# A Mamba block and six local-attention layers in one kernel: the loads of x at the head, the second norm inside the scan, the final sums inside the last layer's slots

## What is computed

```python
# Mamba block, d_inner 256, 16 states
xz, x_gate = x @ W_in + b_in, x @ W_gate + b_gate
act = silu(causal_conv4(xz) + conv_b)
delta = softplus(act @ W_delta + b_delta); Bm, Cm = act @ W_B, act @ W_C
h[t] = exp(delta[t] * A) * h[t-1] + (delta[t] * act[t]) * Bm[t]     # for each channel and state
y[t] = sum_n h[t] * Cm[t] + act * D_skip
x1 = (y * silu(x_gate)) @ W_out + b_out

# six layers, 16 heads of 64, windows of 32 tokens that look one window back
x = attn_layer(shift_tokens(x), ...) + x
x = ffn_layer(shift_tokens(x), ...) + x      # layer norm, W1, gelu gate, W2
```

## Time and profile before

| | us |
|---|---|
| median of three runs | 3793.05 |
| lowest and highest run | 3788.48, 3798.14 |
| the profiled execution: its time | 3797.34 |
| the profiled execution: its span in the trace | 3795.5 |
| from the span's start to the first input projection (PE) | 55.90 |
| first layer's first copy of `xT` (ACT) | 672.93 |
| last `add_y` (DVE) begins | 3779.60 |

### The profile page before, as it was taken

How to read it: one execution, slowest core, us unless ns; L and a number is a source line. 1 busy time by engine, 2 the same in 40 slices (tenths; PEclk the granted TensorE clock), 3 DMA queues, 4 the chain that set the end, 5 groups by cost and what they waited for, 6 DMA issues and landing times.

```text
span 3795.5 us, 148907 instructions
## 1 busy us (share of the span) xinstructions
PE 3526.2 (93%) x61280; PEld 2227.8 (59%) x61280; DVE 3139.4 (83%) x4377; ACT 2647.5 (70%) x4972; POOL 2423.3 (64%) x2197
## 2 busy tenths in 40 slices
PE   5677676899999999999999999999999999999997
PEld 2222222466666666666666666666666666666664
DVE  4899998788888888888878888788888888888883
ACT  4545454677777777777777777777777777777775
POOL 0356555676666666666667676667676666666661
PEclk9889899899999999999999999999999999999998
DMA  3000000011111111111111111011111111111111
GB/s 78 0 0 0 0 0 0 26 34 30 32 37 49 37 32 32 32 49 37 37 33 32 43 43 38 28 32 32 49 41 34 32 32 49 38 37 32 32 32 34
DMA packets 64426, 120.18 MB, mean 32 GB/s; under 512 B 18196, under 2 KB 35986, under 8 KB 63634
## 3 DMA queue, kind: packets, MB, share of 16 engines
q1 hardware_dynamic: 63762, 110.70, 10.0%
HBM read 20.50 MB, written 2.10 MB: 6 GB/s over the span
## 4 chain that ended last, share of the span: by engine, by line
POOL 32%; issue 26%; PE 23%; DVE 1%; ACT 1%; POOLq 1%; DMA 0%; DVEq 0%; ACTq 0%; SPq 0%
POOL arena L501 18%; POOL arena L508 8%; POOL arena L515 6%; PE qk L1132 5%; PE trb L1004 3%; PE ob L1193 3%; PE vob L1201 3%; PE vob L1138 2%; PE sc L1220 2%; PE sc L1169 2%; PE ob L1004 1%; PE sc L1227 1%; PE sc L1163 0%; PE vob L1243 0%; POOL arena L484 0%
## 5 line engine op out<-in xcount | busy, mean ns | idle before, releaser
L508 POOL TENSOR_TENSOR arena<-arena,rnorm 128x512 f32<-128x512 f32 x768 | 786.5, 1046 | 904.0 <-ACT rnorm L627 903.4
L501 POOL TENSOR_TENSOR arena<-arena 128x512 f32<-128x512 f32 x768 | 963.9, 1278 | 36.5 <-DVE arena L889 36.4
L634 ACT ACTIVATE arena<-trb 128x512 f32<-128x512 f32 x768 | 462.6, 602 | 412.9 <-PE trb L1004 412.8
L1132 PE MATMUL qk<-wqkv,xs 128*128 128x512 f32 x1536 | 732.6, 600 | 17.9 <-issue 10.6
L888 DVE TENSOR_TENSOR arena<-qk,tab_q 128x512 f32<-128x512 f32 x384 | 263.5, 686 | 414.7 <-ACT arena L620 407.3
L484 POOL TENSOR_TENSOR arena<-arena 128x512 f32<-128x512 f32 x256 | 300.3, 1183 | 344.3 <-DVE arena L860 328.8
L1004 PE MATMUL trb<-ident,arena 128*128 128x128 f32 x3072 | 483.8, 280 | 14.6 <-ACT arena L634 6.9
L1132 PEld LDWEIGHTS qk<-wqkv,xs 128*128 128x128 f32 x1536 | 293.8, 192 | 311.6 <-issue 295.6
L894 DVE TENSOR_REDUCE ssq<-arena 128x16 f32<-128x1024 f32 x384 | 463.9, 1208 | 0.0
L620 ACT ACTIVATE arena<-qk 128x512 f32<-128x512 f32 x768 | 426.9, 587 | 46.7 <-PE qk L1132 34.1
L1004 PEld LDWEIGHTS trb<-ident,arena 128*128 128x128 f32 x3072 | 347.2, 141 | 147.0 <-issue 99.2
(11 more groups left out here) (139 smaller groups left out, 5862.5 us busy)
## 6 DMA issues: line engine op xcount, KB each, us to landing
arena<-arena SPq DMA_DIRECT2D x192, 384.0 KB, 3.2
arena<-arena SPq DMA_DIRECT2D x192, 64.0 KB, 3.0
wqkv<-in_L_ffn_Wqkv SPq DMA_DIRECT2D x18, 512.0 KB, 3.7
wo<-in_L_ffn_Wo SPq DMA_DIRECT2D x6, 512.0 KB, 5.5
arena<-in_L_attn_x SPq DMA_DIRECT2D x8, 256.0 KB, 2.8
out<-arena SPq DMA_DIRECT2D x8, 256.0 KB, 2.2
w<-in_L_ffn_W SPq DMA_DIRECT2D x6, 341.0 KB, 3.0
arena<-in_sel SPq DMA_DIRECT2D x1, 1024.0 KB, 5.2
```

Of the source, the lines that this page charges most:

```text
L501: nc.gpsimd.tensor_tensor(ts[c * 2 + j][:, heads], tu[:, 0, heads], tu[:, 1, heads], ALU.add).then_inc(summed[0], 1)
L508: nc.gpsimd.tensor_tensor(part, part, rnorm[j][:, 8 * h:8 * h + 8].unsqueeze(2).to_broadcast([P, 8, HEAD]), ALU.mult) \
L634: A((qT, kT)[j][u][:, 4 * h:4 * h + 4, at_col:at_col + P], TRB.rearrange("p (a t) -> p a t", a=4), ACT.Copy) \
L1132: MM(QK[:, 512 * h:512 * h + 512], lhsT=xs[u][:, c * P:(c + 1) * P], rhs=wqkv[:, col:col + 512], start=True, stop=True) \
```

## The change

- **Load.** The identity matrix has a semaphore of its own (`ident_in`) and is loaded first; x follows in eight loads without any wait, each to its own place (`x_tokens`, in the space of `act[0]`) with its own semaphore. The other 25 parameter loads come after. PE waits for the identity and for each block, turns block g into PSUM bank g; the waits for `const_in` move to the first instruction that needs a parameter. ACT's Exp for `a_neg` moves behind the first norm.
- **Second norm.** `NORM_AT` = 14. In the scan of group g the norm of block g - 1 is made in single instructions: `mean_of` on PE at the end of state 13, `centre_output` on DVE at the start of state 14, `square_of` on ACT after the exponentials of state 14, `var_of` on PE after state 15's first step, `root_of` (Ln, Exp) on ACT after the last exponential, `scale_output` on DVE after `gate(g)`. All use bank 7 and one buffer each (`pxc`, `psq`, `prstd`). Only block 7 is left for after the scan.
- **Finish.** `FINAL` names eight slots of the last layer; at the end of such a slot each engine also does its step of `finish` for one block. The buffers are `sq[0]` and `tu`, free after the last unit. From slot 79 on ACT does not load the Exp table again after a gelu (`drain`).

The diff, cut to its core (counts of items shift by 8 where the norms' semaphores lose the second norm's items: that is left out):

```diff
+FINAL = {67: 0, 68: 1, 69: 2, 70: 3, 71: 4, 74: 5, 80: 6, 86: 7}
...
-    for k in range(TURN, LAYER - PER_GROUP + LAG_DOWN + 1):
+    for k in range(TURN, max(FINAL) + 1):
         body(DEPTH - 1, k)
...
-        OUT_AT, D_AT, Z_AT, BC_AT = 2, 5, 9, 13
+        OUT_AT, D_AT, Z_AT, BC_AT, NORM_AT = 2, 5, 9, 13, 14
...
+            sp.dma_start(ident[:], t["ident"]).then_inc(ident_in[0], 16)
+            for g in range(GROUPS):
+                sp.dma_start(x_tokens[g], x_rows[g * GROUP:(g + 1) * GROUP, :].rearrange("(c p) f -> p c f", p=P)).then_inc(x_in[g][0], 16)
             with nc.allow_non_contiguous_dma("small parameters, once"):
                 for dst, src in small:
                     sp.dma_start(dst, src).then_inc(const_in[0], 16)
...
+                g = final_at(l, k)
+                if g is not None:
+                    item(sp, f_ready, g)
+                    sp.dma_start(out_rows[g * GROUP:(g + 1) * GROUP, :].rearrange("(c p) f -> p c f", p=P), xtok[g % 2]).then_inc(f_out[g % 2][0], 16)
...
+            def square_of(j):
+                item(act_e, p_xc, j)
+                A(psq, pxc, ACT.Square).then_inc(p_sq[0], 1)
+
+            def root_of(j):
+                item(act_e, p_var, j)
+                slot(act_e, p_out, j)
+                A(prstd, bank[7][:], ACT.Ln, bias=eps[:, 0:1]).then_inc(p_log[0], 1)
+                item(act_e, p_log, j)
+                A(prstd, prstd, ACT.Exp, scale=-0.5).then_inc(p_rstd[0], 1)
...
+                    if k == NORM_AT * MT + MT - 1 and not first:
+                        square_of(g + -1)
+                if not first:
+                    root_of(g + -1)
...
-                if up0 or up1:
+                drain = isinstance(l, int) and l == DEPTH - 1 and k >= LAYER - PER_GROUP + LAG_UP[0]
+                if up0 or up1 and not drain:
                     act_e.preload_act_table(ACT.Gelu)
...
-                if up0 or up1:
+                if (up0 or up1) and not drain:
                     act_e.preload_act_table_set(EXP_LN_SET)
...
+                    item(act_e, f_turned, g)
+                    if g < 2:
+                        item(act_e, summed, LAST_UNIT * 2 + 1)
+                    else:
+                        act_e.wait_ge(f_out[g % 2][0], g // 2 * 16)
+                    A(xtok[g % 2], bank[g % 2].rearrange("p (c f) -> p c f", f=DIM), ACT.Copy).then_inc(f_ready[0], 1)
...
+            def centre_output(j):
+                item(dve, p_mean, j)
+                item(dve, mo_used, j)
+                V.tensor_tensor(pxc, x1T[:, ds(j * GROUP, GROUP)], bank[7][:], ALU.subtract).then_inc(p_xc[0], 1)
+
+            def scale_output(j):
+                item(dve, g_done, j * MT + (MT - 1))
+                item(dve, p_rstd, j)
+                V.tensor_tensor(xT[:, ds(j * GROUP, GROUP)], pxc, prstd, ALU.mult).then_inc(p_out[0], 1)
...
+                    if n == NORM_AT and not first:
+                        centre_output(g + -1)
                     item(dve, b_ready, g * D_STATE + n)
...
                 gate(g)
+                if not first:
+                    scale_output(g + -1)
...
-            item(dve, mo_used, GROUPS - 1)
-            plain_norm(GROUPS, xT)
+            centre_output(GROUPS - 1)
+            scale_output(GROUPS - 1)
...
+                    item(dve, x_next, (DEPTH - 1) * GROUPS + g)
+                    item(dve, ssq_done, LAST_UNIT)
+                    slot(dve, f_turned, g)
+                    V.tensor_tensor(fin[g % 2], x1T[:, cols], xT[:, cols], ALU.add).then_inc(f_sum[0], 1)
...
+            def mean_of(j):
+                item(pe, mo_used, j)
+                MM(bank[7][:], lhsT=meanw[:], rhs=x1T[:, ds(j * GROUP, GROUP)], start=True, stop=True).then_inc(p_mean[0], 1)
+
+            def var_of(j):
+                item(pe, p_sq, j)
+                MM(bank[7][:], lhsT=meanw[:], rhs=psq, start=True, stop=True).then_inc(p_var[0], 1)
...
                     if 0 <= n - BC_AT < MT and not last:
                         bc_product(g + 1, n - BC_AT)
+                    if n == NORM_AT - 1 and not first:
+                        if not last:
+                            item(pe, z_pos, (g + 1) * MT + 1)
+                        mean_of(g + -1)
+                    if n == NORM_AT + 1 and not first:
+                        var_of(g + -1)
...
+                    item(pe, f_sum, g)
+                    item(pe, roped, LAST_UNIT * 2 + 1)
+                    slot(pe, f_ready, g)
                     for c in range(GROUP // P):
+                        last = turn(bank[g % 2][:, c * P:(c + 1) * P], fin[g % 2][:, c * P:(c + 1) * P], start=True, stop=True)
                     last.then_inc(f_turned[0], 1)
```

More of the change, by code:

```diff
@@ L53, in layer_slots, with final_at @@
             body(l, k)
-    for k in range(TURN, LAYER - PER_GROUP + LAG_DOWN + 1):
+    for k in range(TURN, max(FINAL) + 1):
         body(DEPTH - 1, k)
+def final_at(l, k):
+    return FINAL.get(k) if isinstance(l, int) and l == DEPTH - 1 else None
 def unit_at(l, k, lag):
@@ L221, in build @@
         bc_parts = cut(GROUP // 2).bitcast(bf16)
+        pxc, psq, prstd = (cut(GROUP) for _ in range(3))
         sgate = [xT, xnT]
@@ L235, in build @@
         cleared = sem("cleared")
-        x_in = [sem(f"x_in{u}", 0) for u in range(2)]
-        x_turned = sem("x_turned", 2)
-        x_kept = sem("x_kept", 2)
+        ident_in = sem("ident_in")
+        x_in = [sem(f"x_in{g}") for g in range(GROUPS)]
+        x_turned = sem("x_turned")
+        x_kept = sem("x_kept")
         ln_in = sem("ln_in")
@@ L567, in mamba_in @@
                     A(act[m][:, ds(g * GROUP, GROUP)], cacc[m], ACT.Silu).then_inc(act_done[0], 1)
+            act_e.wait_ge(const_in[0], N_CONST)
+            A(a_neg, a_neg, ACT.Exp).then_inc(a_done[0], 1)
             act_e.preload_act_table(ACT.Silu)
@@ L734, in layer_slot, with with_final @@
                     norms(*unit)
+            def with_final(l, k):
+                layer_slot(l, k)
+                g = final_at(l, k)
+                if g is not None:
+                    item(act_e, f_turned, g)
[4 more added lines that the diff above has]
+                    A(xtok[g % 2], bank[g % 2].rearrange("p (c f) -> p c f", f=DIM), ACT.Copy).then_inc(f_ready[0], 1)
             act_e.wait_ge(cleared[0], 2)
[L737 removed]
+            item(act_e, p_out, GROUPS - 1)
             stage_x(0, 0, 0, 0)
[L739 to L748 removed]
+            layer_slots(act_e, with_final)
         @block.vector
@@ L1004, in turn @@
                 return MM(out_, lhsT=in_, rhs=ident[0:k, 0:k], is_transpose=True, **kw)
-            pe.wait_ge(const_in[0], N_CONST)
-            pe.wait_ge(cleared[0], 1)
-            def load_pair(i):
-                for u in range(2):
-                    pe.wait_ge(x_in[u][0], i * 16 + 16)
-                    slot(pe, x_kept, i * 2 + u)
-                    for c in range(GROUP // P):
-                        last = turn(bank[u][:, c * P:(c + 1) * P], xtok[u][:, c, :], start=True, stop=True)
-                    last.then_inc(x_turned[0], 1)
-            group_loop(pe, 0, GROUPS // 2, load_pair)
+            pe.wait_ge(ident_in[0], 16)
+            for g in range(GROUPS):
+                pe.wait_ge(x_in[g][0], 16)
+                for c in range(GROUP // P):
+                    last = turn(bank[g][:, c * P:(c + 1) * P], x_tokens[g][:, c, :], start=True, stop=True)
+                last.then_inc(x_turned[0], 1)
+            pe.wait_ge(cleared[0], 1)
             def norms_of(i, g0):
@@ L1058, in bc_product, with output_product @@
                     mm.then_inc(bc_done[0], 1)
-            def output_product(g, m, after):
+            def output_product(g, m, after, log=None):
                 if m == 0:
                     item(pe, z_pos, after * MT + 1)
+                    if log is not None:
+                        slot(pe, p_log, log)
                 item(pe, g_done, g * MT + m)
```

128 lines of the change are left out of this document (54 added, 74 removed).

## The result

The changed kernel takes 3767.32 us (median of 4 runs, 3762.99 to 3770.16) and the kernel before 3793.91 on the same chip (4 runs, 3788.48 to 3798.14): a ratio of 0.993, 95% interval 0.9913 to 0.9947, or 26.6 less (20 to 33). Forecast were 3772.5 and the range 3760 to 3784.

A forecast was written before the change was run, and what follows sets the result against it. No single engine at its limit: head bound by a chain of transfers, scan by DVE. Terms -20.3 + 21.0 - 13.8 - 10.2 + 2.8 = -20.5, applied to the median 3793.05, give 3772.5; range 3760 to 3784.

The forecast's parts named there:

- Head, -20.3: Start of kernel: with identity and x loaded first, last turn at 10.9 instead of 31.25, saving 20.3.
- 24.65 left as it is: Head: last copy, norm and handoff from last turn to first input projection stay at 24.65.
- third rival: Head and drain: added work keeps PE's clock up in one norm set and two drain sets, 5.2 less, 3767.3; chance 0.17.
- Norm in the scan, +21.0: Scan: DVE waits 2.0 and runs two more instructions at 0.61 in groups 1 to 6; with group 7, 21.0 more.
- lower bound: Norm in the scan: without any wait, two instructions cost 1.2 a group, 8 in all.
- After the scan, -13.8: From last `add_output` to first copy of `xT`: only block 7 is left, copy at 659.1 instead of 672.93, saving 13.8.
- Finish, -10.2: After the last `add_y`: only block 7 is left, end at 3785.3 instead of 3795.5, saving 10.2.
- Slots 67 to 85, +2.8: Last layer's slots: additions and turns for the seven other blocks delay PE, 2.8 more in all.
- first rival: Scan: DVE regains the wait from its idle time, 10.9 less, giving 3761.6; chance 0.08.
- second: Rival, head: x loads or turns paced by something unseen, or parameters late; gain only 10, giving 3782.8; chance 0.1.
- fourth: Rival, scan: pause at state 14 drops PE to the low clock; eight more low states a group give 3820; chance 0.04.

The follow-up runs named there:

- e11: e2 with 28 long-fulfilled waits on PE put ahead of the loop over the layers: 3802.92 us, ratio 1.0036 to the kernel before.
- e2: Kernel before with only the second norm moved into the scan: 3816.48 us, ratio 1.0065.
- e10: Changed kernel with the loads of x held back to at most two under way, still issued first: 3778.77 us in one run.
- e6: Changed kernel with the mean product one state earlier on PE, ahead of the next group's B/C product: 3755.20 us, ratio 0.9905 to the kernel before.
- e3: Kernel before with only the finish moved into slots of the last layer: 3782.19 us, ratio 0.9971.
- e4: Kernel before with head and finish changed, the second norm left after the scan: 3760.82 us, ratio 0.9912.
- e1: Kernel before with only the head's load order changed: 3770.95 us, ratio 0.9938.
- e12: e2 with the same 28 waits put behind the loop over the layers: 3814.97 us, ratio 1.0065 to the kernel before.
- e7: e6 with POOL instead of DVE scaling the groups in the norm: 3754.28 us, ratio 0.990 to the kernel before.

## Why the prediction was right

The time is within the range and 5.2 below the forecast. That it came so close is in part luck. In the two profiles every stage of the table came out better than forecast, by 3.0, 2.3, 0.4, 8.0 and 0.2, and the spans differ by 34.3 where the forecast's sum is 20.5. The medians differ by 26.6, since before's profiled execution lies above its median and after's below. In the medians of the single parts the misses have both signs: head 2.2 and finish 3.8 more gain than forecast, the norm 5 (e11) to 16 (e2) more loss.

- **Head, -20.3: mechanism right, 3.0 too small.** The transfers had room, as the earlier trace rows said; turning ended at 11.13, where 10.9 for the last turn's start meant 12.0. The "24.65 left as it is" was the wrong step: it contained four passes of 3.78 at the low clock, which became 1.98. That is the first half of the third rival, and e10 shows what goes with it: the gaps between the turns ahead of the norm.
- **Norm in the scan, +21.0: right in mechanism, 18.7.** The wait was forecast at 2.0 and was 1.89, for the reason given (behind the B/C product on PE), and 1.03 in group 7 (forecast 1.1). The group became 69.0, forecast 69.4. That nothing gives it back was right, and e6 shows it: without the wait, 11.9 of the Mamba part go. The rest, two instructions a group at 0.61, was counted a little high: e6 is left with 5.9 over the same stretch of before (602.0 against 596.1), where the lower bound had 8, and 1.0 of it comes back behind the scan (7.7 from the last `add_output` to the first copy in e6, 6.8 in after).
- **After the scan, -13.8: -14.2.** The first copy came 6.0 after the end of the last `add_output`, forecast 6.4. The product's handoff and the two functions took what the rows before said.
- **Finish, -10.2: -10.4.** From the end of the last `add_y` to the end of the span 4.8, forecast 5.0.
- **Slots 67 to 85, +2.8: wrong sign, -3.1 in the profiles** (51.4 against 54.5 from the first of slot 67's values to the last `add_y`). The added steps cost what was said where they can be seen (slot 74: 0.5 more waiting and 0.5 for the turns). Missing was the clock. Before's sets of passes from slot 73 on (eight of the output projection, then four W1 sets) at 3.27, 2.30, 2.56, 3.68 and 3.68 became 1.97, 1.88, 1.98, 1.92 and 1.95: 5.8 less, and +2.8 - 5.8 is what was measured. But this profile of before took longest in the drain, 33.2 from the values of slot 71 to the last `add_y`, where the other five without turns have 29.2 to 31.6. Over all profiles the slots net -1.1 (51.5 against 52.6). The medians agree: e3 gives -11.2 with -10.4 in the tail, about -1, and e4 against e1 about 0. So the term was forecast 3 to 4 too high, because PE's clock in the drain was left as it was.
- **The rivals.** The third, that the added work keeps the clock up, held at 0.17: in the head for certain, in the drain in part. That its number, 3767.3, is the measured median is chance, as the misses above show. I treated it as an alternative to the forecast, though it only changes two of its terms and needed no condition that the change doesn't bring. The first mean passes take 3.78 behind e10's turns with their six gaps and 1.98 behind after's turns with one. The Trainium skill (TensorE: Matmul & The Clock Gate, Part 1) has activity release the throttled clock and idling bring the throttle back; the two traces agree. The scan did not take the wait back (first rival), the head gave all (second), and the scan's clock did not fall: 0.92 in a group, as before (fourth).
- **The whole.** Nothing of the forecast is about the position of code. It was luck that the changed kernel has one pause a turn, like the one before; with e2's placing it could have been about 12 slower, which would have put it near 3779, still inside the range.

## What to carry to other kernels

Work that is moved into a stage whose engine never rests costs its own time plus whatever it waits for, and the wait can be the larger part; look at what the in-order engine that feeds it has in front. One number, the state at which the mean product is issued, was worth 12 of 3767: with it the first layer starts 4.4 earlier than without the move (642.3 against 646.7), and as the change has it 7.5 later. When an edit's parts don't add up, compare the stages that have no edit before explaining those that have one.

## What the runs showed of the hardware

- PE pauses at each turn of this long loop (some 6200 of its instructions), 2.1 to 3.8 us with nothing in the profile to blame. Fourteen instructions more or fewer ahead of the loop decided whether there were one or two such pauses (the two 1.5 to 2.7 each): 12.1 of 3815 here (e11 against e12). Which positions are bad wasn't looked into: 2682 is, 2696, 2700 and 2714 are not.
- The same pause can be followed by passes at the low clock: 3.77 for the first four after a pause of 3.78 in e11, where the granted clock is 0.50, and 2.41 after 2.30 in before, where it is 0.80.
- With four turns (0.65 us) at the end of seven slots of the drain, slot 81's product ran in 1.92 in seven of eight profiles; without them it took 3.68 in five of six.
- A DVE product of 128x512 took 1.15 instead of 0.68 beside a POOL product of the same size (e7 against e6), while the DVE subtraction just before it, also beside POOL's, kept its 0.68.
